# Attention by head groups: row maxima first, then transposed scores that carry the maximum as a 97th row

## The reference

```python
kqv = layernorm(x) @ Wqkv + bqkv                     # q, k, v: 16 heads of 32
scores = einsum('bsnh,btnh->bnst', q, k) / sqrt(32)  # masked above the diagonal with -10000
attn = softmax(scores)                               # over the keys of a query
x = x + (attn @ v) @ Wo + bo
h = layernorm(x)
topk_idx, topk_w = router(h)                         # sigmoid, groups, top 3 groups, top 4 experts
# every token is written into a slot of its experts (dest), at most 320 each
x = x + experts(h, slots) + silu(h @ shared_gate.T) * (h @ shared_up.T) @ shared_down.T
```

## Time and profile before

| | |
|---|---|
| median of 3 runs | 2650.57 us (2649.35 to 2651.34) |
| span of the profiled execution | 2649.2 us |
| `sequences`, from the trace | about 34 to 2222 us |
| a full turn (turn 3 to 15, mean) | 132.0 us |
| turn 16 (no projections) | 115.2 us |
| granted clock of TensorE, mean | 0.967 |

### The profile page before, as it was taken

One profiled execution on the slowest core, in us unless ns is written; L12 is line 12 of the kernel. 1 busy time (PEld: TensorE's weight loads), 2 busy tenths in 40 slices (PEclk: granted clock), 3 DMA queues, 4 the chain that ended last, 5 costly groups with the idle time before them and its releaser, 6 DMA issues. The chain is left out here.

```text
span 2649.2 us, 59186 instructions
## 1 busy us (share of the span) xinstructions
PE 2410.5 (91%) x18327; PEld 1428.9 (54%) x18327; DVE 1791.8 (68%) x6097; ACT 1616.6 (61%) x4166; POOL 774.9 (29%) x993
## 2 busy tenths in 40 slices
PE   5689999999999989999999899989998895999997
PEld 3345555555555555555555555555555553666664
DVE  4466767676767676767676767676767764666664
ACT  4477575757575757575757575757575642666664
POOL 1101213131313131313131313131313134677775
PEclk9799999999999999999999999999999997999999
DMA  4312121212121212121212121212121104788886
GB/s 161 80 50 61 45 73 43 71 46 71 43 71 46 69 45 68 45 70 46 70 46 69 46 67 46 70 44 70 46 69 46 47 33 142 207 230 237 239 227 130
DMA packets 170388, 224.30 MB, mean 85 GB/s; under 512 B 26568, under 2 KB 108592, under 8 KB 170096
## 3 DMA queue, kind: packets, MB, share of 16 engines
q1 hardware_dynamic: 143472, 178.60, 22.3%
q0 software_dynamic: 26624, 42.12, 7.2%
HBM read 113.95 MB, written 56.46 MB: 64 GB/s over the span
## 5 line engine op out<-in xcount | busy, mean ns | idle before, releaser
L612 ACT ACTIVATE S<-S,nmax 128x128 f32<-128x128 f32 (+3 forms) x1024 | 561.6, 551 | 305.9 <-DVE nmax L861 292.7
L962 POOL DMA_INDIRECT slots_dram<-rec,idx x256 | 260.1, 1016 | 1212.9 <-DVE tok L774 1054.4
L861 DVE CUSTOM_DVE_ANT_0 S<-scores,maskrow 128x128 f32<-128x128 f32 (+3 forms) x1024 | 442.4, 488 | 224.2 <-PE scores L490 222.9
L498 PE MATMUL scores<-ident,S 128*128 128x128 f32 x2560 | 454.1, 278 | 61.4 <-ACT S L612 59.7
L619 ACT ACTIVATE pT<-scores 128x128 f32<-128x128 f32 (+3 forms) x1024 | 410.1, 429 | 97.6 <-PE scores L498 91.5
L498 PEld LDWEIGHTS scores<-ident,S 128*128 128x128 f32 x2560 | 324.7, 142 | 218.3 <-ACT S L612 88.5
L490 PE MATMUL scores<-stack_k,stack_q 96*128 96x128 f16 (+3 forms) x1024 | 201.1, 303 | 71.6 <-ACT pT L619 49.7
L513 PE MATMUL o_ps<-pT,v 128*32 128x128 f32 x5120 | 205.4, 291 | 0.7 <-ACT pT L619 0.7
L128 PE MATMUL dense<-xT_hi,wqkv_hi 128*128 128x512 f16 x512 | 196.0, 383 | 1.5 <-DVE xT_lo L827 1.5
L129 PE MATMUL dense<-xT_lo,wqkv_hi 128*128 128x512 f16 x512 | 195.0, 381 | 0.0
L130 PE MATMUL dense<-xT_hi,wqkv_lo 128*128 128x512 f16 x512 | 195.0, 381 | 0.0
(11 more groups left out here) (214 smaller groups left out, 5608.5 us busy)
## 6 DMA issues: line engine op xcount, KB each, us to landing
x2n<-in_x SPq DMA_DIRECT2D x17, 1024.0 KB, 5.5
stack_q<-split_q_hi SPq DMA_DIRECT2D x256, 64.0 KB, 2.0
stack_k<-split_k_hi SPq DMA_DIRECT2D x256, 64.0 KB, 2.0
xres<-in_x SPq DMA_DIRECT2D x16, 1024.0 KB, 5.3
x2n_dram<-x2n SPq DMA_DIRECT2D x16, 1024.0 KB, 4.3
out<-xres SPq DMA_DIRECT2D x16, 1024.0 KB, 4.3
ex_raw_wg<-in_W_gate SPq DMA_DIRECT2D x32, 512.0 KB, 4.1
ex_raw_wu<-in_W_up SPq DMA_DIRECT2D x32, 512.0 KB, 5.0
```

What stands on the lines that cost most here:

```text
L498: last = pe.transpose(ps["scores"][h][:, kt * P:(kt + 1) * P], c["S"][:, h, kt * P:(kt + 1) * P], ident)
L612: act.activation(row, row, ACT.Exp, bias=c["nmax"][:, h:h + 1], scale=-1.0, accum_out=c["den"][:, h:h + 1]).then_inc(exp_done, 1)
L861: dve.tensor_tensor_reduce(out=c["S"][:, h, 0:n], in0=ps["scores"][h][:, 0:n], in1=c["maskrow"][:, SEQ - n:SEQ], scale=-SCALE / (QS * QS), ...
L962: pool.indirect_dma_start(out=a["slots"], out_offset=bass.IndirectOffsetOnAxis(ap=c["idx"][:, t, k:k + 1], axis=0), in_=c["rec"][:, t, k, ...
```

## The change

`GROUPS` is put in another order: q0, k0, the four output projections, the other q and k, v with the transposes of the second norm, router, gate and up, and the transposes `xT` of the next sequence between the down products at the end of the turn. A turn has 125 slots and four **quarters**, one for each head group, that begin at slots 0, 31, 62 and 93 (`QUARTER`). All engines now walk over the same slots.

A head group is worked on twice, a quarter apart. First its scores (L481, in 10 fills of two PSUM banks) and on DVE their row minima (L812, `maxima`); the 16 minima of a row are transposed and cast (L820, L821), and SP places them with 4 DMAs as a 97th row of `stack_q` (row 97 of `stack_k` is a constant). In the next quarter PE makes the **transposed** scores with that row added (L493, 10 fills of two other banks), so that the maximum is subtracted within the product; ACT writes their exponentials straight to `probs`; POOL clears the triangle above the diagonal with `affine_select` (L929, twice four for a head group, at quarter+11 and quarter+20); PE multiplies `probs` with ones for the denominators (quarter+22) and with v (quarter+25), both in `columns`, L502, 512 to 128 columns wide for 4 heads; DVE transposes the denominators in 32x32 blocks, takes the reciprocal, spreads and transposes it back (L826 to L830), scales the 128x512 result (L834), ACT makes its high part and DVE its low part (L838).

The blocks' transposes on PE (L498), those of the reciprocals (L520), ACT's copies `pT` and DVE's work for each step go. The low parts of q and k move from DVE to POOL (`qk_lo`, L921). Stacks are copied for each head group apart (4 times 24 DMAs in a turn). `xres` is one buffer, stored and loaded for each 128 tokens. The scatters are placed one to a slot, from slot 98 to 113. The loop has six passes of two turns (i = 3 to 14). In `setup` the shared weights, the router's and the bias come transposed from the host, and PE's transposes of them go. `experts` is as it was.

The core of the diff:

```diff
-GROUPS = ([g for t in range(TT) for g in (("xT", t, 1), ("out", t, 4))]
-          + [(w, g, 4) for g in range(HG) for w in ("q", "k")]
+GROUPS = ([("q", 0, 4), ("k", 0, 4)] + [("out", t, 4) for t in range(TT)]
+          + [(w, g, 4) for g in range(1, HG) for w in ("q", "k")]
...
-          + [("down", t, 4) for t in range(TT)])
+          + [("xT", 0, 1), ("xT", 1, 1), ("down", 0, 4), ("xT", 2, 1), ("xT", 3, 1)]
+          + [("down", t, 4) for t in range(1, TT)])
+QUARTER = (0, 31, 62, 93)
+FILLS = 10
+ST_SLOT = {base + 2 * f: (q, f) for q, base in enumerate(QUARTER) for f in range(FILLS)}
+S_SLOT = {base + 2 * f + 1: (q, f) for q, base in enumerate(QUARTER) for f in range(FILLS)}
+NM_SLOT = {base + 21: q for q, base in enumerate(QUARTER)}
+TRI_SLOT = {base + at: (q, p) for q, base in enumerate(QUARTER) for p, at in enumerate((11, 20))}
+DEN_SLOT = {base + 22: q for q, base in enumerate(QUARTER)}
+PV_SLOT = {base + 25: q for q, base in enumerate(QUARTER)}
+SCATTER_SLOT = {98 + n: n for n in range(TT * TOPK)}
...
+            def scores_T(s, hg, f):
+                n = (s * HG + hg) * FILLS + f
+                if f == 0:
+                    pe.wait_ge(nm_placed[hg % 2], (s * (HG // 2) + hg // 2 + 1) * NM_DMAS * 16)
+                need(pe, exp_done, n - 1)
+                bank = ps["scores_T"][f % 2]
+                for h, kt, at, cols in ST_FILL[f]:
+                    last = pe.matmul(bank[:, at:at + cols], c["stack_k"][0:SROWS + 1, hg, h, kt * P:(kt + 1) * P],
+                                     c["stack_q"][0:SROWS + 1, hg, h, kt * P:kt * P + cols], start=True, stop=True)
+                last.then_inc(st_done, 1)
+            def columns(left):
+                for kt in range(TT):
+                    for h in range(GH):
+                        n = SEQ - kt * P
+                        last = pe.matmul(ps["o"][h * HD:(h + 1) * HD, kt * P:SEQ], left(kt, h),
+                                         c["probs"][:, h, PCOL[kt]:PCOL[kt] + n], start=kt == 0, stop=kt == TT - 1)
+                return last
+            def denominators(s, hg):
+                n = s * HG + hg
+                pe.wait_ge(tri_done, (n + 1) * 2)
+                pe.wait_ge(exp_done, (n + 1) * FILLS)
+                need(pe, att_done, n)
+                columns(lambda kt, h: c["ones"][:, 0:HD]).then_inc(den_done, 1)
...
+            def triangles(s, hg, p):
+                pool.wait_ge(exp_done, (s * HG + hg) * FILLS + (p + 1) * FILLS // 2)
+                settle(pool)
+                for kt in range(TT):
+                    blk = c["probs"][:, 2 * p:2 * p + 2, PCOL[kt]:PCOL[kt] + P]
+                    last = pool.affine_select(out=blk, in_=blk, compare_op=ALU.is_ge, fill=0.0, base=0,
+                                              pattern=[[0, 2], [1, P]], channel_multiplier=-1)
+                last.then_inc(tri_done, 1)
```

More of the change, by code:

```diff
@@ L542, in _ @@
+            first = before_turn(0)
+            for t in range(TT):
+                dense(-1, 0, [("xT", t, 0, 1, t % DENSE, 0)], first[0:1] if t >= DENSE else [])
             turns(pe, turn)
@@ L546, in _, with copies @@
         def _(act):
[L547 removed]
+            def copies(i, slot, groups):
                 hit = [g for g in groups if g[2] + g[3] - 1 == slot]
@@ L643, in _ @@
             for t in range(TT):
                 norm1(0, t)
+            for t in range(TT):
+                copies(-1, 0, [("xT", t, 0, 1, t % DENSE, 0)])
             turns(act, turn)
```

865 lines of the change are left out of this document (424 added, 441 removed).

## The result

The changed kernel takes **2818.9 us** (2812.4 to 2829.1), the kernel before beside it 2651.0 (2649.4 to 2651.6): a ratio of 1.0644, interval 1.0618 to 1.0669. The forecast had been 2741, the range 2625 to 2805. Slower was right; the loss is 168 us and not 90, and lies beyond the range.

What follows compares the result with a forecast made beforehand. Bound: one ring of DVE, POOL and PE per full turn, 131.8 + 6.6 = 138.4 us, 6.4 over 132.0. Fourteen turns × 6.4 = 90 on 2649.2, plus 1.4, gave 2741 us; range 2625 to 2805.

Steps and rivals of the forecast that it cites:

- The ring: DVE, POOL and PE in one loop of waits per full turn, denominators to denominators: 131.8, with smaller terms 138.4 us.
- POOL's part: From the last destination piece through 15 scatters and eight selects to the denominators at slot 115: 25.1 us.
- DVE's part: From the first routing instruction to the destinations, with row minima, statistics and reciprocals in between: 30.0 us.
- PE's two parts: PE from denominators to the turn's end, 11.2, then slots 0 to 71 with the router, 58.1 and 7.4 us.
- smaller terms: Added to the ring: early denominators 1.0, hand-overs 1.3, jump back 1.8, clock 2.5; 6.6 us a turn.
- Rival 1: Ring shorter: DVE's and POOL's parts under 49 us instead of 55; turn 129.5 to 132, kernel 2614 to 2648; chance 0.25.
- Rival 2: Four heads' 512-column matmuls on PE not fully overlapping: 0.7 us more a product, 4.4 a turn, 2803; chance 0.08.
- Rival 3: A late SP copy holds transposed scores or the load of x: up to 5 us a turn, 2811; chance 0.05.
- Rival 4: No difference within 0.2%, the ring between 131.6 and 132.4 us; chance 0.03.
- Edges together: 0: First two turns +7 us for later stacks, turn 16 −6 for less PE work, setup −2 to 0: together nothing.
- The clock: PE at clock 0.5 after the jump and after its idle before slot 115: 2.5 us a turn, bounds 0 and 4.

Runs made afterwards that it cites:

- experiment 1: Changed kernel with its 16 scatters put behind the fourth quarter's last select, two to a slot: 2707.4 us, ratio 1.0214 to the kernel before.
- experiment 5: Changed kernel with the first norm scales on POOL moved behind the third quarter's last select, the others one slot later: 2766.8 us, one run.
- experiment 10: Changed kernel, statistics behind destinations, x loaded first, first-quarter reciprocals one slot earlier; scatters all behind the last selects 2614.7 us, or two between and fourteen behind 2576.1.
- the kernel with two between: Changed kernel, two scatters between the fourth quarter's selects, fourteen behind; statistics behind destinations, x loaded first, first-quarter reciprocals one slot earlier: 2576.1, again 2579.6 us.
- experiment 6: Changed kernel with the load of the second sequence's x issued ahead of the stack copies, in the first turn alone: 2807.8 us, one run.
- experiment 2: Changed kernel without the 16 scatters of each turn, so its experts stage works on padding: 2658.4 us, one run.

## Why the prediction was right in kind and wrong in size

**Right.** The ring, as it was drawn: it closed at slot 115 with a wait of L502 for L929 of 9.06 (forecast: about 9), and experiment 1 took that wait away. The 15 scatters stood 1.27 to 1.29 apart. POOL's part was 23.9 (25.1). The four selects took 1.48 and not 1.8, so 0.37 for one where 0.45 had been taken between 0.29 and 0.60; and the 2.92 us behind the first scatter, of which half had been put on every turn, stand in two of 16 turns before as after. A 32x32 transpose of 128x512 took 0.71 to 0.72 (0.7). DVE's part was 30.45 once the unforeseen wait was out of it, in experiment 5 (30.0). PE's two parts, 84.5, had been put at 76.7 and 6.6 of smaller terms, 83.3. So the sum of 138.4 meets the 138.7 of experiment 5 in part by luck: PE's parts were 1.2 too short and POOL's 1.3 too long. Waits of PE for DVE's minima were 4.8 in a full turn (7), its idle time 21.0 (24). DVE's sum is 83 in a turn (80); ACT's 49 and POOL's 51, both less than the 55 and 60 forecast.

**Rival 1** (the ring is short) is refuted for the change as made, and experiment 10 meets its condition: with DVE's and POOL's parts at 46.1 together in the kernel with two between, under the 49 that the rival wanted, the kernel is faster. **Rival 2** (four heads not side by side) is refuted: at full clock all 32 records of 512 to 128 columns take 2.36, where three at a time would give 3.1; the four heads' records of 512 columns start 0.007 us apart, and the next four 0.43 behind them. The Trainium skill, "TensorE: Matmul & The Clock Gate", section "Part 3: Packing small matmuls — row/col tiling", has 3.07 times for four row tiles at 512 columns and nothing for four column tiles, which these are; taken for them all the same, it would give an estimated 3.0, and the trace doesn't agree. **Rival 3** (SP's queue) was no cost of full turns, but the place was right for the first turn, in experiment 6. **Rival 4** is excluded by the interval.

**Wrong, in three places.** The forecast was 6.4 more for each of 14 full turns and nothing for the edges. Measured were 9.8 for each of 13, and 34.1 outside them.

1. *The ring's sum left out the selects of the third quarter.* The working for DVE's part named the statistics at 4.2 us and said that DVE is late there, but it did not go on to ask which of POOL's instructions are queued behind the scales that wait for them. Experiment 5 gives 2.8 a turn, and with it a ring of 138.7; the forecast had said 138.4. Thirteen intervals at 3.4 too little are 44 us; experiment 5 accounts for 37 of them, the other 7 belong to no single term.
2. *"Edges together: 0".* They were +12.8 up to the first routing instruction, +5.3 and +16.0 at the end, where only the fourteenth turn's 6.4 were forecast: 28 us too little. The working had seen the load of x behind the stacks and gave it 7 for two turns; experiment 6 shows 5 for it. The larger part of the 12.8 is the wait of step 1 once more, in turn 1: experiment 5 took 8.8 away. Against the 7 the working had set a gain of 6 in turn 16, where PE has less work. But PE's work doesn't set turn 16: PE's last denominators wait 17.0 us there for the same 15 scatters, since the ring's DVE and POOL parts are 27.5 and 25.6. Without the scatters (experiment 2) the last two distances are 108.6 and 69.6, below the 116.1 and 71.3 of before. To count a shorter engine as a gain in the one place and not in the rest was the error.
3. *The clock.* The loss after a wait was foreseen (2.5, bounds 0 and 4), and one mean was taken for it. In the full turns the clock stands at 0.5 for 174 us in 26 stretches, before for 75 in 15. At half clock half of the time is lost (2.36 us become 4.50), so up to 50 us more, 3.8 a turn, if all of it is on the path. How much of it is on the path was not measured apart; some of it is within the 44 us of step 1, since behind the third quarter's wait the denominators took up to 4.5. The loss also varies: the four executions had 0.936 to 0.944 and 2812 to 2829 us, the slowest with the lowest clock, where those of before lie 2 us apart. The profiled one was the fastest, 6.6 below the median.

The first two make the 72 us by which the span of the profiled execution, 2810.6, exceeds its forecast of 2739. The other 6 of the 78 come in because the profiled execution was the fastest of four, and go with the clock, the third. The range was too narrow for the same reason: its upper end took in prices of instructions, and no second wait.

## What to carry to other kernels

When a queue gets an instruction that another engine waits for, list everything ahead of it on that queue, and for each of these what it waits for in turn; do so for every place where the instruction stands, not only for the one with the longest queue. Work without a reader in the turn, here 16 scatters and four norms' scales, belongs behind such an instruction, and must then be weighed as a load on the start of the next turn: moving the scatters and the statistics together took back 157 of the 168 us, while the second of the two moves alone made the kernel slower. The kernel got ahead of the one before only with smaller steps on top: 44 us with the load and the first quarter's reciprocals moved (not separated here), 39 with two scatters put into POOL's idle stretch between the selects. An edge turn in which one engine has less to do is shorter only if that engine sets the turn.

## What the runs showed of the hardware

- Fp32 matmuls in four groups of 32 columns of the array run side by side for 512 columns: their records start 0.007 us apart, the next four 0.43 later; 16 matmuls (32 records), 1280 columns for each head, take 2.36 us at full clock and 4.50 at 0.50.
- PE at the granted clock 0.5 follows idle times of 3.75 us in some turns and not in others: the third quarter's denominators took 2.4 in turns 7 and 8 and 4.5 in turns 11 to 14, behind the same wait of 3.8. Behind 9 us they took 3.7 to 4.5 in every turn. A shorter wait can be enough: behind 2.0 to 2.3 us the first quarter's value product took 3.6 to 4.1 in five of the turns 3 to 14, with the clock at 1.00 up to the wait, and 2.36 in the other seven.
- A 128x512 fp32 transpose in 32x32 blocks on DVE takes 0.72, a select over 128x2x128 on POOL 0.37, a scatter on POOL's queue 1.27 to 1.29 from start to start where it is followed by another.
- One scatter of a turn stands behind an idle time of 2.9 us, and not 0.30, in two of 16 turns: before (the one of the earlier trace rows and at 2139.8), in the changed kernel (1311.7 and 2285.3) and in experiment 1 (1286.1 and 2199.4). No cause was found.
- On two occasions the kernel before took 2661 to 2663 and not 2649 to 2651, and one new kernel 2712 where it took 2583 elsewhere. There DVE idled for 7.6 to 10.5 us once in each full turn, at the same instruction, with no semaphore of this core as releaser; in the execution of 2579 never. What made it stays open.
